# The opening of an AdaLN transformer block: order and size of the first loads, layout of the query and key copies, constant rows by DMA

## The reference

```python
x = L0_attn_x                                   # (4, 1024, 256), float32
mod = (silu(c) @ wmod).reshape(4, 6, 1, 256)    # sa, ca, ga, sb, cb, gb
ga, gb = sign * max(abs, 0.25)
h = layernorm(x) * (1 + ca) + sa
qkv = h @ W_qkv.T + b_qkv                       # 16 heads of 16
attn = softmax(Q @ K.T / 4 + causal)            # t = 1024
x = x + ga * ((attn @ V) @ W_o.T + b_o)
h = layernorm(x) * (1 + cb) + sb
# mixture of experts: 8 experts, the top 2 of a router, silu between w1 and w2
x = x + gb * sum_of_top2(combine * (silu(h @ w1[e]) @ w2[e]))
```

## Time and profile before

| | |
|---|---|
| median of 3 runs | 989.07 us (988.89 to 993.22) |
| the profiled execution's own time, first to last instruction (the span) | 985.5 us |
| instructions | 19308 |
| mean granted TensorE clock | 0.975 of full speed |
| moved by DMA | 110.61 MB |
| VectorE, ScalarE, GpSimd busy | 712.9, 580.1, 350.7 us |

### The profile page before, as it was taken

The page is one execution under the profiler, slowest core; times in us unless marked ns, Lnnn a source line. Parts: engine busy times, 40 slices in busy tenths (PEclk is TensorE's granted clock), DMA queues, the critical chain, the costliest instruction groups (busy, mean ns, idle before and its releaser), DMA issues.

```text
span 985.5 us, 19308 instructions
## 1 busy us (share of the span) xinstructions
PE 890.2 (90%) x6090; PEld 529.1 (54%) x6164; DVE 712.9 (72%) x2285; ACT 580.1 (59%) x1268; POOL 350.7 (36%) x311
## 2 busy tenths in 40 slices
PE   7899899998899999989999987888899999999990
PEld 4443335433535434544443453432798899999880
DVE  7898776879566889657689668899547575444588
ACT  3335676766676777586676757757535433333563
POOL 4200030530430324323023444024585465565530
PEclk8998999999999999999999999999999999999996
DMA  6484535525506336253464565105332323222699
GB/s 204 122 176 108 79 110 111 91 72 98 79 1 144 68 79 144 76 70 95 73 123 105 127 114 180 36 26 177 110 97 76 96 73 105 73 81 75 194 313 306
DMA packets 83235, 110.61 MB, mean 112 GB/s; under 512 B 15930, under 2 KB 56434, under 8 KB 83138
## 3 DMA queue, kind: packets, MB, share of 16 engines
q1 hardware_dynamic: 75234, 88.40, 38.2%
q0 software_dynamic: 6816, 18.62, 6.0%
q10 hardware_dynamic: 1088, 2.36, 0.6%
HBM read 69.42 MB, written 35.41 MB: 106 GB/s over the span
## 4 chain that ended last, share of the span: by engine, by line
PE 64%; DVE 17%; ACT 9%; issue 6%; POOL 3%; DMA 1%; another core or an unknown queue 1%; SPq 0%; ACTq 0%; DVEq 0%; POOLq 0%
PE PY L1608 10%; PE PO L1741 9%; PE PH L1608 9%; PE PM L1698 9%; PE PS L1721 8%; ACT PR L1073 3%; PE PHT L1826 3%; DVE MXF L1410 3%; DVE JK L1407 3%; PE PX L1753 2%; PE PX L1662 2%; PE PS L1725 2%; PE PX L1673 1%; PE PX L1770 1%; POOL SF L912 1%
## 5 line engine op out<-in xcount | busy, mean ns | idle before, releaser
L1073 ACT ACTIVATE PR<-PS 128x512 f32<-128x512 f32 (+3 forms) x768 | 335.3, 499 | 125.6 <-PE PS L1725 85.6
L1407 DVE CUSTOM_DVE_ANT_0 JK<-PM,MK 128x128 bf16<-128x128 f32 (+3 forms) x512 | 239.5, 485 | 54.9 <-PE PM L1698 52.5
L1698 PE MATMUL PM<-QK 128*128 128x512 bf16 (+3 forms) x725 | 234.3, 332 | 22.9 <-DVE MXF L1410 11.6
L1721 PE MATMUL PS<-QK 128*128 128x512 bf16 (+3 forms) x737 | 235.0, 330 | 11.7 <-ACT PR L1073 9.2
L1410 DVE TENSOR_REDUCE MXF<-PM 128x1 f32<-128x512 f32 x256 | 175.2, 684 | 76.8 <-PE PM L1698 61.0
L1721 PEld LDWEIGHTS PS<-QK 128*128 128x128 bf16 x768 | 75.5, 99 | 167.2 <-ACT PR L1073 105.3
L1741 PE MATMUL PO<-PR,V 128*17 128x512 f32 (+3 forms) x1536 | 162.3, 495 | 0.2 <-DVE MXA L1407 0.2
L1698 PEld LDWEIGHTS PM<-QK 128*128 128x128 bf16 x768 | 75.5, 98 | 94.7 <-DVE MXF L1410 33.6
L1608 PE MATMUL PY<-W2S,HT 128*128 x852 | 119.4, 289 | 2.6 <-issue 1.8
L1725 PE MATMUL PS<-MT,identb 128*128 128x128 bf16 x512 | 111.4, 220 | 1.6 <-issue 0.8
L1608 PE MATMUL PH<-W1S,XT 128*128 x426 | 111.7, 397 | 0.6 <-DVE W2S L1562 0.6
(11 more groups left out here) (282 smaller groups left out, 1159.2 us busy)
## 6 DMA issues: line engine op xcount, KB each, us to landing
QK<-SD SPq DMA_DIRECT2D x180, 128.0 KB
SD<-SP SPq DMA_DIRECT2D x42, 256.0 KB, 2.9
OP<-OS SPq DMA_DIRECT2D x64, 64.0 KB
LP<-LR SPq DMA_DIRECT2D x64, 64.0 KB
W1S<-in_w SPq DMA_DIRECT2D x8, 512.0 KB, 6.6
X<-XA SPq DMA_DIRECT2D x3, 1024.0 KB, 8.4
H2D<-XA SPq DMA_DIRECT2D x3, 1024.0 KB, 4.8
YG<-YT SPq DMA_DIRECT2D x12, 256.0 KB
```

The lines of the kernel that those rows point to most:

```text
L1073: eng.activation(PR[:, slot, i, c0:512], PS[m % 3][:, c0:512], ACT.Exp, scale=0.25).then_inc(S["exp"].sem, 1)
L1407: eng.tensor_tensor_reduce(JK[:, jk % 2, 0:w], PM[m % 3][:, 0:w], MK[:, 512 - w:512], 1.0, -3.0e38, ALU.add, ALU.max, MXA[:, mb, h, qt:qt ...
L1698: eng.matmul(PM[m % 3][:, 0:128 * (k1 - k0)], QK[:, r, h, 0, qt * 128:(qt + 1) * 128], QK[:, r, h, 1, k0 * 128:k1 * 128], start=True, stop ...
L1721: last = eng.matmul(PS[m % 3][:, c0:512], QK[:, r, h, 1, j * 128:(j + 1) * 128], QK[:, r, h, 0, 512 * f + c0:512 * f + 512], start=True, s ...
```

## The change

- x of batch 0 is loaded in three parts: tiles 0 and 1 (SP), 2 and 3 (ACT), 4 to 7 (SP). `WM0` comes in two halves, one on each queue. SP loads x of batch 1 only when W has landed; ACT loads `WM1` after the first transposes' evacuation.
- The columns of W that make queries and keys, and their bias, are permuted on the host by indexing, so that in `SD` the row of a part is `8 r + h` and no longer `16 h + r`. `SD` has the order (unit, which, place, row, token); keys are stored with their parts in the reverse order. Three reads now fill the six blocks of a kind: one of 16, one of 32 and one of 48 partitions.
- Stores wait and go by kind: all parts of the queries, then all of the keys (`sd` has a fourth member, `which`). For heads 8 to 15 they stand at steps -21 and -18, before at -9.
- Constant rows: only rows 96 to 98 (`KR` = 99 rows take part in the products). POOL sets them in one slot, after `trd`, and two DMAs copy them to the other slots. DVE's two memsets at the start are gone, and its other clearing stands behind the V steps.
- Warm-up products: 8 instead of 16, and three more behind `trd`.
- Of the first four tiles ACT normalizes one and DVE three (two and two before). The first projection waits for each half of hT separately.
- V of tiles 4 to 7 moves from the opening to the steps 4 and 6 of group 0; `NEXT_QK` and `MOD2_AT` move.

```diff
-WARM = 16
+WARM = 8
+KR = 99
-MOD2_AT = -20
-NEXT_QK = (-32, -36, -29, -22)
-SD1_AT, REP2_AT = -9, -5
+MOD2_AT = -18
+V0_AT = 4, 6
+NEXT_QK = (-29, -24, -22, -20)
+SD1_AT, REP2_AT = (-21, -18), -5
...
-ROWS = [(which, n, part) for which, parts in enumerate(((0, 0, 0, 1, 1, 2), (0, 1, 2, 0, 1, 0)))
-        for part in range(3) for n in range(6) if parts[n] == part]
+ROWS = [(which, n, first, many) for which, firsts in enumerate(((0, 0, 0), (2, 1, 0))) for n, first, many in zip((5, 3, 0), firsts, (1, 2, 3))]
...
-        steps = stat[:4] + [("root", 0, 0), ("norm", 0, 0, 0), ("norm", 0, 0, 1), stat[4], ("mod",), ("clear",), ("tr", 0, 0, 0), ("trd",)]
-        steps += stat[5:] + [first[0], ("root", 0, 1), *first[1:3], ("norm", 0, 1, 0), *first[3:], ("norm", 0, 1, 1)]
-        steps += [("v", 0, 0), ("v", 0, 1), ("sd", 0, 0), ("rep", 0, 0)]
+        steps = stat[:4] + [("root", 0, 0), ("norm", 0, 0, 0), ("norm", 0, 0, 1), ("mod",), ("tr", 0, 0, 0), ("trd",)]
+        steps += stat[4:] + [first[0], ("root", 0, 1), *first[1:3], ("norm", 0, 1, 0), *first[3:], ("norm", 0, 1, 1)]
+        steps += [("v", 0, 0), ("v", 0, 1), ("clear",), ("sd", 0, 0, 0), ("sd", 0, 0, 1), ("rep", 0, 0)]
         steps += [("stat", 1, n) for n in range(NT)] + [("tr", 0, 0, 1), ("tr", 0, 1, 1)] + second
-        steps += [("v", 0, 2), ("v", 0, 3), ("sd", 0, 1), ("rep", 0, 1)]
-        return steps + [("root", 1, 2)]
+        return steps + [("sd", 0, 1, 0), ("sd", 0, 1, 1), ("rep", 0, 1), ("root", 1, 2)]
...
+    for tp, k in zip((2, 3), V0_AT):
+        place(0, k, one("v", 0, tp))
...
-            for half, name in enumerate(("ld_xa", "ld_x0")):
-                eng.dma_start(xt(4 * half, 4 * half + 4),
-                              x[0, 512 * half:512 * half + 512].rearrange("(t p) d -> p t d", p=128)).then_inc(S[name].sem, 16)
+            eng.dma_start(xt(0, 2), x[0, 0:256].rearrange("(t p) d -> p t d", p=128)).then_inc(S["ld_xa"].sem, 16)
+            eng.dma_start(WM0[:, 0, :], wmod[0:128, 0:512]).then_inc(S["wm0"].sem, 16)
+            eng.dma_start(xt(4, 8), x[0, 512:1024].rearrange("(t p) d -> p t d", p=128)).then_inc(S["ld_x0"].sem, 16)
             eng.dma_start(BQ[:, :], b_qk).then_inc(S["ld_bq"].sem, 16)
+            sp.wait_ge(S["ld_w"], 16)
...
+                eng.dma_start(QK[16 * n:16 * (n + many), r, :, which, sl],
+                              SD[u, which, first:first + many, :, sl].rearrange("s (r h) t -> (s r) h t", h=8)[:, h0:h0 + 4, :]
                               ).then_inc(S["rep_a" if half == 0 else f"rep{r}"].sem, 16)
...
+                    if (g, half) == (0, 0):
+                        sp.wait_ge(S["neg_p"], 2)
+                        for i in (1, 2):
+                            eng.dma_start(QK[96:KR, slot_of(i), :, :, :], QK[96:KR, slot_of(0), :, :, :]).then_inc(S["neg"].sem, 16)
...
                     sp.wait_ge(*after("cd", "crow", g, f))
+                    sp.wait_ge(S["neg"], 33)
...
                 elif kind == "clear":
-                    for g in (1, 2):
-                        for which, value in ((0, 0.0), (1, TWO_MINUS_ONES)):
-                            turn("neg_p")
-                            eng.memset(QK[96:128, slot_of(g), :, which, :].bitcast(F32), value).then_inc(S["neg_p"].sem, 1)
+                    po.wait_ge(*after("mod", "trd"))
+                    for which, value in ((0, 0.0), (1, TWO_MINUS_ONES)):
+                        turn("neg_p")
+                        eng.memset(QK[96:KR, slot_of(0), :, which, :].bitcast(F32), value).then_inc(S["neg_p"].sem, 1)
...
-            eng.memset(QK[96:128, slot_of(0), :, 0, :].bitcast(F32), 0.0).then_inc(S["neg"].sem, 1)
-            eng.memset(QK[96:128, slot_of(0), :, 1, :].bitcast(F32), TWO_MINUS_ONES).then_inc(S["neg"].sem, 1)
...
+                    for n in range(3):
+                        eng.matmul(PM[2][:, :], identb[:, :], MK[:, :], start=True, stop=True)
...
-                eng.matmul(PM[m % 3][:, 0:128 * (k1 - k0)], QK[:, r, h, 0, qt * 128:(qt + 1) * 128],
-                               QK[:, r, h, 1, k0 * 128:k1 * 128], start=True, stop=True).then_inc(S["m"].sem, 1)
+                eng.matmul(PM[m % 3][:, 0:128 * (k1 - k0)], QK[0:KR, r, h, 0, qt * 128:(qt + 1) * 128],
+                               QK[0:KR, r, h, 1, k0 * 128:k1 * 128], start=True, stop=True).then_inc(S["m"].sem, 1)
...
+    rows = np.arange(512).reshape(4, 8, 16).transpose(0, 2, 1).reshape(512)
```

More of the change, by code:

```diff
@@ L184, in schedule @@
         if u:
-            place(*((0, SD1_AT) if u == 1 else (2 * u - 3, 23)), one("sd", u, 2))
+            for which in range(2):
+                place(*((0, SD1_AT[which]) if u == 1 else (2 * u - 3, (16, 23)[which])), one("sd", u, 2, which))
         if u < 2 * B - 1:
@@ L319 @@
 NR = len(ROUTE[0])
-LATE = ()
 RING = 10
@@ L656, in sub_done, with sd_done @@
             lane.wait_ge(*after("sub_d" if key[0] == 0 else "sub_p", stage, *key))
-        def sd_done(lane, u, part, half=2):
-            lane.wait_ge(*after(f"sd{part}", "sd", u, half if u else min(half, 1)))
-            if u == 0 and part == 0:
-                lane.wait_ge(*after("wm0", "sd", 0, 0))
+        def sd_done(lane, u, which, half=2):
+            lane.wait_ge(*after(f"sd{which}", "sd", u, half if u else min(half, 1), which))
         def xt(n0, n1):
@@ L706, in store @@
                 sl = slice(512 * (half == 1), T - 512 * (half == 0))
-                name = "wm0" if (u, half, part, which) == (0, 0, 0, 0) else f"sd{part}"
-                eng.dma_start(SD[u, part, which, :, sl], SP[:, part, which, sl]).then_inc(S[name].sem, 16)
+                place = 2 - part if which else part
+                eng.dma_start(SD[u, which, place, :, sl], SP[:, part, which, sl]
+                              ).then_inc(S[f"sd{which}"].sem, 16)
             for step in order:
@@ L743, in sync_program @@
                 elif kind == "sd":
[L744 to L756 removed]
+                    u, half, which = a
+                    for part in range(3):
+                        store(u, half, part, which)
                 elif kind == "crow":
@@ L817, in sync_program @@
                             sp.wait_ge(*after("pv", "pv", NG - 5, 1, 7))
-                            for part in range(3):
-                                sd_done(sp, 2 * B - 1, part)
+                            for which in range(2):
+                                sd_done(sp, 2 * B - 1, which)
                             sp.wait_ge(*after(f"rep{slot_of(NG - 1)}", "rep", NG - 1, 2))
@@ L864, in gpsimd_program @@
             const = S["const"].sem
-            done = {n: 0 for n in ("const", "sub_p", "neg_p", "gbo", "div_p", "om", "bias", "h2", "both", "cmb_p")}
+            done = {n: 0 for n in ("const", "sub_p", "neg_p", "gbo", "div_p", "om", "bias", "h2", "both")}
             newest = []
@@ L1668, in tensor_program @@
                     pe.wait_ge(S["ld_w"], 16)
-                    turned(pe, u // 2, half)
+                    pe.wait_ge(*after("hT", "tr", u // 2, 0, half))
                     step = ("qk", *a)
@@ L1707, in tensor_program @@
                 elif kind == "bvo":
-                    pe.wait_ge(*after("bvb", "bvb"))
+                    pe.wait_ge(*after("bvo", "bvb"))
                     px_free(pe, step)
```

94 lines of the change are left out of this document (37 added, 57 removed).

## The result

| | before | after |
|---|---|---|
| median of the runs | 988.98 us (983.45 to 993.22, 8 runs) | 994.39 us (990.69 to 999.35, 8 runs) |
| profiled execution: span | 985.5 us | 989.0 us |
| mean granted clock, median of the runs | 0.972 (of the 29 runs beside experiment 1) | 0.9625 |

What follows compares the result with a forecast made beforehand. The opening's chain changes hands between VectorE and TensorE, then DMA, until group 1's scores at 105.86 us. -6.4 + 3.5 + 0.8 + 0.9 = -1.2 us: span 984.3, median 987.9, range 981.8 to 992.3.

Steps and rivals of the forecast that it cites:

- Step 1: Opening until the first row maximum: VectorE and POOL stalls go, maximum at 30.15, -6.4 us, bounds 8.0 and 3.5 us gain.
- rival B: Opening: another resource sets the first maximum, nearest TensorE at half clock from the start; +1.0, 990.1 us; chance 0.13.
- Step 2: V of tiles 4 to 7, moved to group 0's steps 4 and 6, is paid there: +3.5 us, between 0 and 4.3.
- Rival A: Group 0, steps 4 and 6: V is hidden in its new place; -5.6 or -5.2, 983.9 us; chance 0.24.
- Steps 3 and 4: Four next-head projections among the maxima, +0.8 us; TensorE's clock falling around the first maximum, +0.9, between 0 and 2.6.
- step 3: Next heads' projections, all four now among the maxima: 0 to 1.7 us plus 0 to 1 for casts; taken +0.8.
- Rival C: TensorE stays at half clock through most of the first 17 steps, two falls of 2.6 us; +4.0, 993.1; chance 0.11.
- Step 5: Reads, constant-row copies, early query stores, added wait and 99 rows in the products: zero, between -1 and +1 us.

Runs made afterwards that it cites:

- experiment 1: Four kernels on one chip: changed kernel with 128 rows, V elsewhere or more warm-up; kernel before with 99 rows: medians 989.35, 994.50, 996.83 and 990.58 us.
- a_warm16: Changed kernel with 16 instead of 8 warm-up products: 996.83 us, ratio 1.0084 to the kernel before.
- l_v46: Changed kernel with 128 rows and the kernel before's places for projections, second modulation and query stores; V stays at steps 4 and 6: 986.68 us, ratio 0.9994.
- l_best: Changed kernel with 128 rows, V of tiles 4 to 7 in the opening, projections, second modulation and query stores at their old places: 985.90 us, ratio 0.9977.
- b_clear: Kernel before with only the constant rows' new setting by POOL and DMA, still rows 96 to 127: 987.61 us, ratio 0.9988.
- l_six: Changed kernel with 128 rows, V in the opening, projections, second modulation and query stores at old places, six reads a kind: 990.33 us, ratio 1.0019.
- l_six_sd23: Changed kernel with 128 rows, V in the opening, old projection places, six reads a kind, later heads' queries stored at step 23: 990.57 us, ratio 1.0020.
- b_max64: Kernel before with the products for the maxima over rows 0 to 63 alone, scores over all 128: 1105.66 us, ratio 1.1158.
- b_rows99: Kernel before with both kinds of products over rows 0 to 98 instead of 0 to 127: 990.58 us, ratio 1.0024.

## Why the prediction was wrong

**Step 1, the first maximum: right in its mechanism, mis-sized.** I said -6.4; it was -4.55, within the bounds that I gave. The stalls on VectorE and POOL went as worked out. Late was TensorE. The modulation began at 7.84 and not at 6.8, since it waited for its weights, and took 3.55 us and not 1.84. That is the beginning of my rival B: behind eight warm-up products the pace is still that of the lower level. VectorE ended its evacuation at 14.04, 3.0 us after my 11.0, and made up 1.2 of this, 0.7 of it in the clearing, which I charged with 1.9 and which took 1.2 (21.46 to 22.67). By the Trainium skill (TensorE: Matmul & The Clock Gate, Part 1: The HAM clock gate), which I had quoted for this rival, the clock starts low and work lifts it; the trace agrees in the pace, 3.55 against 1.84 us for the same sixteen columns. But a_warm16 says that mending it gains nothing that can be measured.

**Step 2, V of tiles 4 to 7: right in its mechanism.** +3.5 forecast, 3.1 in the traces from the first score on, 1.7 to 4.0 in the times. VectorE's two new waits for TensorE, 1.12 and 1.35 us, are where I expected them. Rival A is refuted as to V. But that V costs nothing in its old place is not sure: l_v46 and l_best differ by only 1.2 us at group 1.

**Steps 3 and 4, projections and clock: right in sign, too small.** I gave them 0.8 and 0.9, and bounded step 3 by 2.7. From the first maximum to the first score the change lost 2.6 us, with the forecast fall of the clock in 32 to 39 (0.51). Of the stretch to group 1 the places cost 1.4 more, which I had not counted at all since I looked no further than 54. With step 1's shortfall this makes the +2.3 us at group 1 against my -1.2. Rival C's price was two falls of 2.6 us; of it one longer fall is left, 32 to 39 at 0.51, and 39 to 54.8 reads 1.00. What my sum lacked besides is that the gain at the first maximum need not arrive at the first score: with the places of the kernel before it is 22.40 us between the two in l_best and 23.46 in b_clear, against 20.25, with the wait for GpSimd shown above.

**Step 5 failed: "99 rows instead of 128 in 1536 products: the trace has no product with fewer rows. Zero, between -1 and +1 for all of this."** Two things in it were far outside these bounds, with opposite signs. The 99 rows cost 2.4 to 6.5 us. The work takes the same time by its records, and I had the record in mind, not the clock. What decides here is the clock: after the change its mean is 0.9625, with 128 rows in the same kernel 0.9755. The Trainium skill (TensorE: Matmul & The Clock Gate, Why this matters for your kernels) says that a single product of 32 rows takes the time of one of 128. By that rule alone the rows would be free; the trace agrees as to the single product, 391 ns for 512 columns with 99 rows as with 128. That fewer rows lower the clock is shown by the four pairs, in all of which it is 0.0075 to 0.016 lower over the runs; why they do is not shown. And three reads for six gained 3.6 to 4.9 us in kernels with the new order of rows. I had argued that their time is hidden, since TensorE's weight loads wait 0.7 us for DMAs in the whole program. That row counts only direct waits: the row sums of a batch stand behind the reads on SP, and whoever waits for them waits for another engine's name. This is the way seen once, in l_six; that it carries all of the gain is not shown. Nor is it shown that three reads beat the kernel before's own six: every pair has the new order of rows on both sides. From the copy of group 1's maxima to the last one it is 554.4 us in the kernel before (six reads, old order), 554.8 in l_best (three, new) and 557.3 in l_six (six, new), so the new order may have made six reads dearer and three of them only made this good. One execution each does not settle it, since b_clear, with the reads of the kernel before, takes 557.5.

**The sum.** The two errors of step 5 nearly cancel, and what went otherwise up to group 1 (steps 1 to 4) accounts for 3.5 us. My -1.2 with these 3.5 and with the means of the rows' and the reads' shares (+4.3 and -4.2) would be +2.4, and +6.5 was measured. The difference lies behind group 1 and is not settled: l_six_sd23, which differs from the kernel before in the repeating part only by the order of rows within a head's tile and of the stores by kind, starts group 1 1.5 us earlier (104.38) and is 2.0 us slower (0 to 4.0). Either of these edits, or the later waits that come with them, may cost about 3.5 us. This figure carries 2 us of scatter, and the difference of 4.1 us between +6.5 and +2.4 carries 3. They were not tried alone. I had taken the row order as free without saying so.

My own mark for being wrong, "if the time per group from there on differs from before", is what happened. The best version found, l_best, is faster than both kernels, by little: 0.9952 and 0.9977 in its two measurements, with intervals that end at 0.9977 and 0.9992.

## What to carry to other kernels

Cutting the contraction rows of the products that fill TensorE saved it no time here, and it lowered the clock that it was granted: compare the mean granted clock of several runs before and after such an edit, not the durations. In l_six no engine waited for the reads by name, and yet a small round trip queued behind twelve of them stood on the chain: to call a transfer hidden, follow its queue's timeline too, as a row of direct waits misses what is passed on by another engine. Work moved out of an opening is charged nearly in full where TensorE has no idle time, as V was here with 3.1 us. And an earlier start is worth only what arrives at the next fixed point: 4.1 us at the first maximum of b_clear were 0.9 at its first score.

## What the runs showed of the hardware

Products with 64 rows between products with 128 are dear. In b_max64 the maxima's weight loads are as short as ever (93 ns), but they are issued late: 181.6 us of idle time stand before them, 101.7 of it in which nothing is waited for that the profile shows.

```profile
L1698 PEld LDWEIGHTS PM<-QK 64*128 64x128 bf16 x768 | 70.4, 93 | 181.6 <-issue 101.7 <-DVE MXA L1407 41.3 <-DVE MXF L1410 25.7
```

In the kernel before it is 94.7 and 8.2, and in b_rows99 96.1 and 8.2:

```profile
L1698 PEld LDWEIGHTS PM<-QK 128*128 128x128 bf16 x768 | 75.5, 98 | 94.7 <-DVE MXF L1410 33.6 <-DVE MXA L1407 20.2 <-issue 8.2
```
```profile
L1698 PEld LDWEIGHTS PM<-QK 99*128 99x128 bf16 x768 | 75.8, 99 | 96.1 <-DVE MXF L1410 34.4 <-DVE MXA L1407 20.6 <-issue 8.2
```

The scores' loads, which still have 128 rows in b_max64, have 104.1 us of such time before them against 46.8. The timelines show how. In the kernel before the next weights start loading with the product before them, and the next product starts 0.21 us after it. In b_max64 they start 0.31 us after it, when it is nearly over, and the next product starts 0.32 us after it. The first pair is from the kernel before, the second from b_max64 (start, us):

```profile
302.43 0.38 PE L1698 MATMUL PM<-QK 128*128 128x512 bf16 x1
302.43 0.10 PEld L1721 LDWEIGHTS PS<-QK 128*128 128x128 bf16 x1
...
302.64 0.38 PE L1721 MATMUL PS<-QK 128*128 128x512 bf16 x1
```
```profile
331.93 0.39 PE L1698 MATMUL PM<-QK 64*128 64x512 bf16 x1
...
332.24 0.10 PEld L1721 LDWEIGHTS PS<-QK 128*128 128x128 bf16 x1 [0.23 <-issue]
332.25 0.39 PE L1721 MATMUL PS<-QK 128*128 128x512 bf16 x1
```

The time rose by 11.6%, 114 us. So fewer rows had two costs here, one in the clock, seen at 99, and one in the overlap of weight loads, seen at 64 beside 128 and not at 99. The mixture of two numbers is not enough for the second: in b_rows99 the products of the causal mask keep all 128 rows, and their weights start at 300.55 us beside a 99-row product that started at 300.54. Where between 64 and 99 it begins was not tried, nor 64 rows in both kinds of products.
